# Attention in a one-core decoder kernel: turning the scaled numerators alone, and adding the turned queries behind the turn

## The chip, the cores and the metric

The kernel runs on one core of one Trainium2 chip. A core has five engines with queues of their own: TensorE (PE, with its weight loads shown as PEld), VectorE (DVE), ScalarE (ACT), GpSimd (POOL) and SyncE (SP, which here issues DMAs). They meet through semaphores. The metric is the time on the device in microseconds, as the median of several runs; lower is better.

## What is computed

A decoder block over x of shape (16, 112, 256) and a context of shape (16, 375, 256): four RWKV layers, a cross attention with softmaxed queries and keys, and eight gated experts. The change lies in the cross attention:

```
q = softmax(heads(x @ Wq.T + bq), axis=-1)
k = softmax(heads(y @ Wk.T + bk), axis=-1)
v = heads(y @ Wv.T + bv)
k_cumsum = sum(k, axis=-2, keepdims=True)
D_inv = 1.0 / sum(q * k_cumsum, axis=-1, keepdims=True)
kv = einsum("bhnd,bhne->bhde", k, v)
out = q + einsum("bhnd,bhde->bhne", q, kv) * D_inv
return out @ Wp.T + bp
```

There are 16 batches of 112 queries, 16 heads of 16 columns, 256 channels.

## The kernel before

Every engine has one program, written out by hand in a fixed order, and a semaphore wait stands wherever one engine needs another. An instruction that waits holds back all that is behind it in its engine's queue.

The attention part (attention_phase) runs a loop over the 16 batches n. In each round the context of a batch is projected to keys and values, the keys are softmaxed (VectorE: maxima L1178, arguments L1182; ScalarE: exponential L1410; VectorE: sum, reciprocal and product, L1187 to L1189), and TensorE forms the product of keys and values (keys_values, L1575) in the bank kvp, which VectorE copies into block diagonal matrices (L1156, L1158). The queries go in groups c of four batches (G = 4). stage(n) gives the place i = n % 4, the group c1 whose queries are being made and the group c2 = c1 - 1 whose attention is being made. For a group c2 the steps are:

- round i = 3 of the queries' own group: TensorE turns the queries q into the bank qbanks (q_turned), and ScalarE copies them to qt (L1399). They are turned so that they can be the stationary side of the next products.
- round i = 0: TensorE forms denominators (L1530) and numerators (L1535, into abanks); VectorE takes the reciprocal of the denominators (L1232).
- round i = 1: VectorE scales the numerators to num (L1239) and adds them to the queries, q (L1241). Then it makes the arguments of the next group's queries (L1216, L1220). TensorE, at the end of its round, turns the sum into abanks (turn_out, L1512), and ScalarE copies it to ot (L1403).
- round i = 2: TensorE projects ot with wp into abanks (project_out, L1519 and the bias L1474).
- round i = 3: VectorE adds the result to x (L1245), and the statistics of a layer norm follow.

ot is the same memory as xt, which holds the turned x for the query projection, so its rows in a profile bear the name xt. Behind round 15 a tail finishes the last group beside the first products of the experts (times_up: hf, L1820; low_h: hl, L1827; silu, L1925). From about 896 us TensorE works through the experts.

Of the kernel before, what the change touches and what calls it, by code (L numbers as in the profile page):

```python
# [8 lines left out]
ACT = mybir.ActivationFunctionType  # L9
# [3 lines left out]
B, T, C = 16, 112, 256  # L13
L, F = 4, 1024
CB = C // P
G = 4
# [948 lines left out]
def attention_phase(nc, g, io, ctx):  # L965
# [6 lines left out]
    with tiles:  # L972
# [133 lines left out]
        def vector(dve):  # L1106
            steps = [0]

            def did(ins):
                ins.then_inc(dve_step, 1)  # L1110
                steps[0] += 1
                return steps[0]

            def after(n):
                dve.wait_ge(dve_step, n)
# [7 lines left out]
            def heads(t):  # L1123
                return t.rearrange("p t (h d) -> p (t h) d", d=D)

            def head_banks(banks):
                return banks[0:T].rearrange("p i (h d) -> p (i h) d", d=D)

            def spread(t):
                return t[:].unsqueeze(2).broadcast_to([t.shape[0], t.shape[1], D])  # L1130
# [82 lines left out]
            def q_arguments(c):  # L1213
                qc = q[c % 2][:]
                dve.wait_ge(q_done, c + 1)
                after(did(dve.tensor_reduce(qtop[:], head_banks(qbanks), AX.X, ALU.max)))  # L1216
                if c >= 2:

                    dve.wait_ge(o_turned, CB * (c - 1))
                dve.tensor_tensor(heads(qc), head_banks(qbanks), spread(qtop), ALU.subtract).then_inc(qarg_ready, 1)  # L1220

            def q_normalise(c):
# [10 lines left out]

            def attend(c):

                qc = q[c % 2][:]
                dve.wait_ge(den_read, c + 1)
                dve.wait_ge(num_done, c + 1)
                after(did(dve.tensor_tensor(heads(num[:]), head_banks(abanks), spread(drec), ALU.mult)))  # L1239
                dve.wait_ge(q_turned, CB * (c + 1))  # L1240
                dve.tensor_tensor(qc, qc, num[:], ALU.add).then_inc(o_ready, 1)  # L1241

            def add_attention(c):
                dve.wait_ge(pj_done, c + 1)
# [27 lines left out]
            def groups():  # L1272

                times_up, low_h, combine_arguments, combine_weights, experts = g["expert"]["vector"](dve)
                dve.wait_ge(mask_set, 3)
                for n in range(B):
                    i, c1, c2 = stage(n)
                    k_arguments(n)
                    if n == 0:
                        output_bias()  # L1280
                    if n:
                        block_diagonals(n - 1)
                    if i == 0 and c1 is not None:
                        add_input(c1)
                    if i == 2 and c1 is not None:
                        q_normalise(c1)
                    if i == 3 and c2 is not None:
                        add_attention(c2)
                    k_normalise(n)
                    if n + 2 < B:  # L1290
                        low_context(n + 2)
                    if i == 0 and c1 is not None:
                        rsqrt(1, c1)
                    if i == 0 and c2 is not None:
                        denominators(c2)
                    if i == 1 and c2 is not None:
                        attend(c2)
                    if i == 1 and c1 is not None:
                        q_arguments(c1)
                    if i == 3 and c2 is not None:  # L1300
                        rsqrt(2, c2)
                    if n in SPLITS:
                        low_weights(SPLITS.index(n))
                    if i == 2 and n in TURNS:
                        low_x2(TURNS.index(n))
                last = GROUPS - 1
                times_up(0, 0, 0)
                times_up(0, 0, 1)
                block_diagonals(B - 1)
                low_h(0, 0)  # L1310
                low_x2(last - 1)
                denominators(last)
                attend(last)
                for n in (2, 3):
                    times_up(0, 0, n)
                    low_h(0, n - 1)
                add_attention(last)
                times_up(0, 1, 0)
                low_h(0, 3)
                rsqrt(2, last)  # L1320
                times_up(0, 1, 1)
                low_h(0, 4)
                low_x2(last)
                times_up(0, 1, 2)
                low_h(0, 5)
                times_up(0, 1, 3)
                combine_arguments()
                low_h(0, 6)
                combine_weights()
                experts()  # L1330
# [3 lines left out]
        def scalar(act):  # L1334
# [57 lines left out]
            def groups():  # L1392

                silu, high_h, combine_exp, experts = g["expert"]["scalar"](act)
                last = GROUPS - 1

                def q_turned_out(c):
                    act.wait_ge(q_turned, CB * (c + 1))
                    act.activation(qt[c % 2][:], qbanks[:, :, 0:G * T], ACT.Copy).then_inc(qt_ready, 1)  # L1399

                def o_turned_out(c):
                    act.wait_ge(o_turned, CB * (c + 1))
                    act.activation(ot[:], abanks[:, :, 0:G * T], ACT.Copy).then_inc(ot_ready, 1)  # L1403

                act.wait_ge(const_set, 4)
                v_out(0)
                for n in range(B - 1):
                    i, c1, c2 = stage(n)
                    act.wait_ge(arg_ready, n + 1)
                    act.activation(k[n % 2][:], k[n % 2][:], ACT.Exp).then_inc(exp_ready, 1)  # L1410
                    if n in TURNS:
                        x2_out(TURNS.index(n))
                        high_x2(TURNS.index(n))
                    if n + 2 < B:
                        high_context(n + 2)
                    if i == 0 and c1 is not None:
                        rsqrt0(1, c1)
                    if i == 3 and c2 is not None:
                        rsqrt0(2, c2)
                    if i == 3 and c1 is not None:  # L1420
                        q_turned_out(c1)
                    v_out(n + 1)
                    if i == 1 and c1 is not None:
                        act.wait_ge(qarg_ready, c1 + 1)
                        act.activation(q[c1 % 2][:], q[c1 % 2][:], ACT.Exp).then_inc(qexp_ready, 1)
                    if i == 1 and c2 is not None:
                        o_turned_out(c2)
                    if i == 0 and c1 is not None:
                        normalise(1, c1, x1_ready)
                        act.wait_ge(x1_turned, CB * (c1 + 1))  # L1430
                        act.activation(xt[:], qbanks[:, :, 0:G * T], ACT.Copy).then_inc(xt_ready, 1)
                    if i == 3 and c2 is not None:
                        normalise(2, c2, x2_ready)
                    if n + 1 in SPLITS:
                        high_weights(SPLITS.index(n + 1))
                act.wait_ge(arg_ready, B)
                act.activation(k[(B - 1) % 2][:], k[(B - 1) % 2][:], ACT.Exp).then_inc(exp_ready, 1)
                q_turned_out(last)
                rsqrt0(2, last - 1)
                silu(0, 0, 0)  # L1440
                normalise(2, last - 1, x2_ready)
                silu(0, 0, 1)
                high_h(0, 0)
                x2_out(last - 1)
                high_x2(last - 1)
                silu(0, 0, 2)
                high_h(0, 1)
                o_turned_out(last)
                silu(0, 0, 3)
                high_h(0, 2)  # L1450
                silu(0, 1, 0)
                high_h(0, 3)
                rsqrt0(2, last)
                normalise(2, last, x2_ready)
                silu(0, 1, 1)
                high_h(0, 4)
                act.wait_ge(g["r_done"], 1)
                logits_out(act, kvp, g, EARLY)
                x2_out(last)
                high_x2(last)  # L1460
                silu(0, 1, 2)
                high_h(0, 5)
                silu(0, 1, 3)
                act.wait_ge(g["r_done"], 2)
                logits_out(act, kvp, g, LATE)
                high_h(0, 6)
                combine_exp()
                experts()
# [3 lines left out]
        def tensor(pe):  # L1472
# [83 lines left out]

            def turn_out(c):
                pe.wait_ge(o_ready, c + 1)
                turn(abanks, q[c % 2], o_turned)

            def project_out(c):
                pe.wait_ge(ot_ready, c + 1)
# [587 lines left out]
```

## Time and profile before

| | us |
|---|---|
| runs | 1817.99, 1819.19, 1819.70 |
| median | 1819.19 |
| the profiled execution | 1819.54 |
| its span | 1817.5 |
| TensorE busy | 1730.9 (95%) |
| VectorE busy | 1222.5 (67%) |
| ScalarE busy | 986.7 (54%) |

The times of a profile are counted from the start of its span; the 2 us beside it lie around the program. A timeline row says when an instruction, or a row of like ones, started, how long it took, on which engine and line of the kernel, and what it wrote from what. In square brackets is the time that the engine had been idle before it, with the instruction that released it. The ends of matmuls are modelled. VectorE and ScalarE start an instruction that doesn't depend on the one before shortly before that one's end.

### The profile page before, as it was taken

To read this page: it belongs to the slowest core of one execution; us is meant where nothing else is said; L and a number is where in the kernel's file an instruction comes from. 1 tells how busy PE (TensorE), PEld (TensorE's weight loads), DVE (VectorE), ACT (ScalarE), POOL (GpSimd) and SP (SyncE) were. 2 spreads that over 40 slices of the span, in tenths; PEclk is the share of its full clock that TensorE was granted. 3 is DMA by queue.
4 is the path that set the end of the run, shared out by engine and by line. 5 is a ranking of instruction groups with operands and counts; after the bars stand their busy time and mean duration, and the time that the engine had idled before them with its cause. 6 is when DMAs were issued, how large, how long until landed. Compare 5 with 4: busy or idle time off the path is not lost.

```text
span 1817.5 us, 27302 instructions
## 1 busy us (share of the span) xinstructions
PE 1730.9 (95%) x10508; PEld 1514.4 (83%) x10508; DVE 1222.5 (67%) x1897; ACT 986.7 (54%) x1516; POOL 18.6 (1%) x42
## 2 busy tenths in 40 slices
PE   3599999999999898989999999999999999999997
PEld 1388888878888788988899989998899989999896
DVE  6989999999999856998454544444454444545446
ACT  4789998998999773455533332333332333333324
POOL 1000000000000000000000000000000000000000
PEclk9699999999999999999999999999999999999999
DMA  7301110011011002111111001110111101020001
GB/s 187 58 1 30 24 59 18 18 29 65 12 24 41 1 29 90 45 55 50 52 36 36 27 9 35 35 35 0 35 35 35 35 0 35 35 75 0 1 1 41
DMA packets 37966, 64.79 MB, mean 36 GB/s; under 512 B 3286, under 2 KB 22012, under 8 KB 36860
## 3 DMA queue, kind: packets, MB, share of 16 engines
q1 hardware_dynamic: 34620, 55.47, 9.4%
q0 software_dynamic: 3264, 8.19, 3.0%
q8 instruction: 55, 0.90, 0.2%
q14 instruction: 27, 0.22, 0.0%
HBM read 59.99 MB, written 3.67 MB: 35 GB/s over the span
## 4 chain that ended last, share of the span: by engine, by line
PE 82%; DVE 8%; ACT 6%; issue 2%; DMA 2%; SPq 0%; ACTq 0%; POOL 0%; DVEq 0%; POOLq 0%
PE fbank L1998 34%; PE fbank L2020 17%; PE pair L882 8%; PE pair L867 7%; PE pair L842 7%; PE pair L852 5%; PE proj L1480 2%; PE pair L832 1%; ACT kf L659 1%; ACT kfh L661 1%; DMA wckl<-in_w_ck 1%; PE qbanks L1519 1%; PE abanks L1519 1%; DMA x<-in_ln_b 1%; ACT kf L657 1%
## 5 line engine op out<-in xcount | busy, mean ns | idle before, releaser
L1820 DVE TENSOR_TENSOR hf<-sil,fbank 128x512 f32<-128x512 f32 (+1 forms) x256 | 158.9, 621 | 478.9 <-PE fbank L1998 407.3
L1925 ACT ACTIVATE sil<-fbank 128x512 f32<-128x512 f32 (+1 forms) x256 | 139.3, 544 | 614.6 <-PE fbank L1998 614.6
L1998 PE MATMUL fbank<-xh,wh 128*128 128x512 f32 (+1 forms) x1024 | 290.0, 365 | 1.2 <-ACT sil L1925 1.2
L1998 PE MATMUL fbank<-xh,wl 128*128 128x512 f32 (+1 forms) x1024 | 288.9, 363 | 0.0
L1998 PE MATMUL fbank<-xl,wh 128*128 128x512 f32 (+1 forms) x1024 | 288.8, 363 | 0.0
L2020 PE MATMUL fbank<-wl,hh 128*128 128x256 f32 x896 | 250.3, 279 | 0.0
L2020 PE MATMUL fbank<-wh,hh 128*128 128x256 f32 x896 | 250.2, 279 | 0.0
L2020 PE MATMUL fbank<-wh,hl 128*128 128x256 f32 x896 | 250.1, 279 | 0.0
L1998 PEld LDWEIGHTS fbank<-xl,wh 128*128 128x128 f32 x1024 | 184.6, 189 | 30.9
L1998 PEld LDWEIGHTS fbank<-xh,wl 128*128 128x128 f32 x1024 | 184.4, 189 | 30.3
L1998 PEld LDWEIGHTS fbank<-xh,wh 128*128 128x128 f32 x1024 | 180.6, 189 | 27.8 <-ACT sil L1925 1.6
L2020 PEld LDWEIGHTS fbank<-wl,hh 128*128 128x128 f32 x896 | 168.3, 188 | 2.1
L2020 PEld LDWEIGHTS fbank<-wh,hh 128*128 128x128 f32 x896 | 168.4, 188 | 1.8
L2020 PEld LDWEIGHTS fbank<-wh,hl 128*128 128x128 f32 x896 | 168.4, 188 | 0.0
L1827 DVE TENSOR_TENSOR hl<-hf,hh 128x512 fp32r<-128x512 f32 (+1 forms) x256 | 158.3, 618 | 0.0
L882 PE MATMUL pair<-wcvh,kfh 128*112 128x256 f32 x512 | 147.2, 287 | 0.0
L1918 ACT ACTIVATE hh<-hf 128x512 fp32r<-128x512 f32 (+1 forms) x256 | 146.3, 571 | 0.5 <-DVE hf L1820 0.5
L882 PE MATMUL pair<-wcvh,kfl 128*112 128x256 f32 x512 | 143.3, 280 | 0.0
L882 PE MATMUL pair<-wcvl,kfh 128*112 128x256 f32 x384 | 107.6, 280 | 0.0
L882 PEld LDWEIGHTS pair<-wcvh,kfh 128*112 128x112 f32 x512 | 89.8, 175 | 0.7
L882 PEld LDWEIGHTS pair<-wcvh,kfl 128*112 128x112 f32 x512 | 89.8, 175 | 0.0
L1844 DVE SCALAR_TENSOR_TENSOR acc<-fbank,cw,acc 128x256 f32<-128x256 f32 x210 | 87.5, 477 | 0.0
(240 smaller groups left out, 3096.8 us busy)
## 6 DMA issues: line engine op xcount, KB each, us to landing
raw<-in_w_gate SPq DMA_DIRECT2D x16, 512.0 KB, 3.8
raw<-in_w_up SPq DMA_DIRECT2D x16, 512.0 KB, 4.7
raw<-in_w_down SPq DMA_DIRECT2D x16, 512.0 KB, 5.8
raw<-in_w_ck SPq DMA_DIRECT2D x4, 1024.0 KB, 6.6
raw<-in_w_cv SPq DMA_DIRECT2D x4, 1024.0 KB, 6.9
wcvl<-in_w_cv POOLq DMA_DIRECT2D x6, 512.0 KB, 5.4
raw<-in_ctx_t SPq DMA_DIRECT2D x4, 750.0 KB, 5.9
ct<-in_ctx_t SPq DMA_DIRECT2D x4, 750.0 KB, 4.9
```

Source lines behind the costliest of these rows:

```text
L842: ins = pe.matmul(pair[BANKS[name]][:, o, 0:G * T], w[:, b, o * P:(o + 1) * P], mixed[name][:, b].rearrange("p g t -> p (g t)"), start=b = ...
L852: ins = pe.matmul(banks[0:T, i // 2, (i % 2) * C:(i % 2 + 1) * C], src[:, b, i, :], w[:, b, :], start=b == 0, stop=b == CB - 1)
L867: ins = pe.matmul(banks[:, i, 0:G * T], w[b], a[:, b, :], start=n == 0, stop=n == 3 * CB - 1)
L882: ins = pe.matmul(pair[3][0:T, i // 2, (i % 2) * C:(i % 2 + 1) * C], a[:, i * T:(i + 1) * T], w, start=j == n == i % 2 == 0, stop=j == FT ...
L1480: ins = pe.matmul(proj[0:ST, out, :], a[s % 2][:, b, t * ST:(t + 1) * ST], w[:, b, cols], start=n == 0, stop=n == 3 * CB - 1 and cols.star ...
L1820: dve.tensor_tensor(hf[i][:, 0:w], sil[i][:, 0:w], banks(e, t, f)[1][:, 0:w], ALU.mult).then_inc(hf_ready, 1)
L1827: dve.tensor_tensor(hl[t % 2][:, f, 0:w], hf[f % 2][:, 0:w], hh[t % 2][:, f, 0:w], ALU.subtract)\
L1844: ins = dve.scalar_tensor_tensor(a, ps, w, a, ALU.mult, ALU.add)
L1918: act.activation(hh[t % 2][:, f, 0:w], hf[f % 2][:, 0:w], ACT.Copy).then_inc(hh_ready, 1)
L1925: act.activation(sil[f % 2][:, 0:w], banks(e, t, f)[0][:, 0:w], ACT.Silu).then_inc(sil_ready, 1)
L1998: ins = pe.matmul(banks(e, t, f)[k][:, 0:w], m[h][:, o:o + P], a[:, b, columns(c)], start=i == 0, stop=i == 3 * CB - 1)
L2020: ins = pe.matmul(bank[4 + 2 * (t % 2) + i // 2][:, (i % 2) * C:(i % 2 + 1) * C], a[t % 2][:, f, i * P:(i + 1) * P], m[h][:, DOWN + f * C: ...
```

## The change

The queries are no longer added before the turn. VectorE scales the numerators to num, and TensorE turns num alone. Since the queries lie turned in qt already, VectorE then adds qt to the turned numerators out of abanks and writes ot itself (add_query, with 128 x 896 elements). ScalarE's copy o_turned_out is gone. Four waits follow from that:

- the scaling of a group waits until num has been turned for the group before (o_turned);
- the new addition waits for the turn (o_turned) and for the copy of the queries (qt_ready);
- the arguments of a later group's queries wait for q_turned where they waited for o_turned;
- ScalarE's copy of the turned queries waits for the addition that read that buffer last (ot_ready).

```
@@ vector: q_arguments
-                    dve.wait_ge(o_turned, CB * (c - 1))
+                    dve.wait_ge(q_turned, CB * (c - 1))
@@ vector: attend
-                qc = q[c % 2][:]
                 dve.wait_ge(den_read, c + 1)
                 dve.wait_ge(num_done, c + 1)
-                after(did(dve.tensor_tensor(heads(num[:]), head_banks(abanks), spread(drec), ALU.mult)))
-                dve.wait_ge(q_turned, CB * (c + 1))
-                dve.tensor_tensor(qc, qc, num[:], ALU.add).then_inc(o_ready, 1)
+                if c:
+                    dve.wait_ge(o_turned, CB * c)
+                dve.tensor_tensor(heads(num[:]), head_banks(abanks), spread(drec), ALU.mult).then_inc(o_ready, 1)
+            def add_query(c):
+                dve.wait_ge(o_turned, CB * (c + 1))
+                dve.wait_ge(qt_ready, c + 1)
+                dve.tensor_tensor(ot[:], abanks[:, :, 0:G * T], qt[c % 2][:], ALU.add).then_inc(ot_ready, 1)
@@ vector: groups
                     if i == 1 and c1 is not None:
                         q_arguments(c1)
+                    if i == 1 and c2 is not None:
+                        add_query(c2)
...
                 attend(last)
-                for n in (2, 3):
-                    times_up(0, 0, n)
-                    low_h(0, n - 1)
+                times_up(0, 0, 2)
+                add_query(last)
+                low_h(0, 1)
+                times_up(0, 0, 3)
+                low_h(0, 2)
@@ scalar
                     act.wait_ge(q_turned, CB * (c + 1))
+                    if c >= 2:
+                        act.wait_ge(ot_ready, c - 1)
                     act.activation(qt[c % 2][:], qbanks[:, :, 0:G * T], ACT.Copy).then_inc(qt_ready, 1)
-                def o_turned_out(c):
-                    act.wait_ge(o_turned, CB * (c + 1))
-                    act.activation(ot[:], abanks[:, :, 0:G * T], ACT.Copy).then_inc(ot_ready, 1)
...
-                    if i == 1 and c2 is not None:
-                        o_turned_out(c2)
...
-                o_turned_out(last)
@@ tensor: turn_out
-                turn(abanks, q[c % 2], o_turned)
+                turn(abanks, num, o_turned)
```

VectorE's queue in round 5, where group 0 has its place i = 1; acl is the low half of a context, the k and top rows belong to the keys of the next batch. Before:

```order
L1169 TENSOR_TENSOR acl<-ct,ach 128x2x375 [waits proj_done,acth_ready]
L1239 TENSOR_TENSOR num<-abanks,drec 112x1024 [waits num_done,den_read]
L1241 TENSOR_TENSOR q<-q,num 112x1024 [waits q_turned,adve_step]
L1216 TENSOR_REDUCE qtop<-qbanks 112x64 [waits q_done]
L1220 TENSOR_TENSOR q<-qbanks,qtop 112x1024 [waits adve_step]
L1178 TENSOR_REDUCE top<-proj 125x48 [waits v2_ready,proj_done]
L1182 TENSOR_TENSOR k<-proj,top 125x768 [waits kv_done,adve_step]
```

and now:

```order
L1169 TENSOR_TENSOR acl<-ct,ach 128x2x375 [waits proj_done,acth_ready]
L1241 TENSOR_TENSOR num<-abanks,drec 112x1024 [waits num_done,den_read]
L1216 TENSOR_REDUCE qtop<-qbanks 112x64 [waits q_done]
L1220 TENSOR_TENSOR q<-qbanks,qtop 112x1024 [waits adve_step]
L1247 TENSOR_TENSOR xt<-abanks,qt 128x896 [waits qt_ready,o_turned]
L1178 TENSOR_REDUCE top<-proj 125x48 [waits v2_ready,proj_done]
L1182 TENSOR_TENSOR k<-proj,top 125x768 [waits kv_done,adve_step]
```

The addition has moved from ahead of the query arguments to behind them, right ahead of the next batch's maxima, and waits there for TensorE's turn.

VectorE's queue in the tail, group 3; hf and hl are the experts' hidden values and their low half. Before:

```order
L1232 RECIPROCAL drec<-kvp 112x64 [waits den_done]
L1239 TENSOR_TENSOR num<-abanks,drec 112x1024 [waits num_done,den_read]
L1241 TENSOR_TENSOR q<-q,num 112x1024 [waits q_turned,adve_step]
L1820 TENSOR_TENSOR hf<-sil,fbank 128x512 [waits hh_ready,hl_ready,gu_done,sil_ready]
L1827 TENSOR_TENSOR hl<-hf,hh 128x512 [waits hh_ready]
```

and now:

```order
L1232 RECIPROCAL drec<-kvp 112x64 [waits den_done]
L1241 TENSOR_TENSOR num<-abanks,drec 112x1024 [waits o_turned,num_done,den_read]
L1826 TENSOR_TENSOR hf<-sil,fbank 128x512 [waits hh_ready,hl_ready,gu_done,sil_ready]
L1247 TENSOR_TENSOR xt<-abanks,qt 128x896 [waits qt_ready,o_turned]
L1833 TENSOR_TENSOR hl<-hf,hh 128x512 [waits hh_ready]
```

Here the addition stands behind the first of the two products. TensorE's queue keeps its order; its turns read num where they read q.

## Rows read from the trace of the kernel before

**Rows 1.** The page's busy times, and busy times of 760 to 780 us
```profile
PE 1730.9 (95%) x10508; PEld 1514.4 (83%) x10508; DVE 1222.5 (67%) x1897; ACT 986.7 (54%) x1516; POOL 18.6 (1%) x42
...
core 0: us, PE busy (x) PEld busy (x) DVE busy (x) ACT busy (x) POOL busy (x), PEclk, DMA share, GB/s
...
760.00:780.00 20.00, 18.80 (x147) 17.78 (x146) 19.52 (x31) 10.39 (x19) 0.00 (x0) 1.00 0.17 52
```

**Rows 2.** Timeline of VectorE, group 0: start, duration, line, out<-in
```profile
752.87 1.22 DVE L1239 TENSOR_TENSOR num<-abanks,drec 112x1024 f32<-112x1024 f32 x1
754.12 1.23 DVE L1241 TENSOR_TENSOR q<-q,num 112x1024 f32<-112x1024 f32 x1
755.26 1.22 DVE L1216 TENSOR_REDUCE qtop<-qbanks 112x64 f32<-112x1024 f32 x1
756.51 1.23 DVE L1220 TENSOR_TENSOR q<-qbanks,qtop 112x1024 f32<-112x1024 f32 x1
757.65 0.95 DVE L1178 TENSOR_REDUCE top<-proj 125x48 f32<-125x768 f32 x1
```

**Rows 3.** Timeline of TensorE, group 0: the turn, and the projection's first products
```profile
757.68 0.93 PE L1512 MATMUL abanks<-ident,q 112*128 112x112 f32 x8
...
759.89 1.02 PE L1519 MATMUL abanks<-wp,xt 128*112 128x256 f32 x4
```

**Rows 4.** Timeline of TensorE, behind group 0: two waits for VectorE
```profile
774.47 1.61 PE L1575 MATMUL kvp<-v,k 125*128 125x129 f32 x12 [0.55 <-DVE k L1189]
...
785.49 1.60 PE L1575 MATMUL kvp<-v,k 125*128 125x129 f32 x12 [0.59 <-DVE drec L1232]
```

**Rows 5.** Timelines of VectorE and TensorE, group 1
```profile
797.82 0.95 DVE L1178 TENSOR_REDUCE top<-proj 125x48 f32<-125x768 f32 x1
...
807.60 0.94 DVE L1169 TENSOR_TENSOR acl<-raw,ach 128x750 fp32r<-128x750 f32 x1 [2.10 <-ACT ach L1382]
...
797.84 0.93 PE L1512 MATMUL abanks<-ident,q 112*128 112x112 f32 x8
```

**Rows 6.** Timelines of VectorE and TensorE, group 2
```profile
841.17 0.95 DVE L1178 TENSOR_REDUCE top<-proj 125x48 f32<-125x768 f32 x1
...
847.89 0.96 DVE L1189 TENSOR_TENSOR k<-k,rec 125x768 f32<-125x768 f32 x1
850.24 1.09 DVE L1253 TENSOR_TENSOR xl<-acc,xh 128x896 fp32r<-128x896 f32 x1 [1.40 <-ACT xh L1367]
851.52 0.96 DVE L1178 TENSOR_REDUCE top<-proj 125x48 f32<-125x768 f32 x1 [0.19 <-PE proj L1474]
...
841.20 0.93 PE L1512 MATMUL abanks<-ident,q 112*128 112x112 f32 x8
...
858.92 0.73 PE L1998 MATMUL fbank<-xh,wh 128*128 128x512 f32 x2 [1.19 <-ACT sil L1925]
```

**Rows 7.** Timelines of VectorE and TensorE, the tail with group 3
```profile
869.82 0.69 DVE L1820 TENSOR_TENSOR hf<-sil,fbank 128x512 f32<-128x512 f32 x1 [0.27 <-PE fbank L1998]
...
869.60 0.99 PE L1512 MATMUL abanks<-ident,q 112*128 112x112 f32 x8
...
873.18 1.02 PE L1519 MATMUL abanks<-wp,xt 128*112 128x256 f32 x4
```

**Rows 8.** By tile: durations in ns (min/median/max), first and last start, forms
```profile
L1239 DVE TENSOR_TENSOR num<-abanks,drec x4: 1217/1218/1225, 752.9 to 867.1; 112x1024 f32<-112x1024 f32 x4
L1403 ACT ACTIVATE xt<-abanks x4: 902/902/920, 758.7 to 870.6; 128x896 f32<-128x896 f32 x4
...
L1253 DVE TENSOR_TENSOR xl<-acc,xh x4: 1085/1093/1093, 809.6 to 890.5; 128x896 fp32r<-128x896 f32 x4
```

**Rows 9.** TensorE's granted clock (PEclk) in stretches, and rows before and in one
```profile
705.79 1.90 PE L1575 MATMUL kvp<-v,k 125*128 125x129 f32 x12 [3.02 <-DVE k L1189]
709.62 1.75 PE L1512 MATMUL qbanks<-ident,x 112*128 112x112 f32 x8 [1.93 <-ACT x L1354]
...
708.00:712.00 4.00, 2.38 (x12) 2.39 (x13) 1.70 (x4) 2.16 (x5) 0.00 (x0) 0.50 0.00 0
...
814.00:818.00 4.00, 2.29 (x19) 2.08 (x19) 3.90 (x7) 2.22 (x6) 0.00 (x0) 1.00 0.02 4
```

## The prediction

> **What bounds the kernel now.** I read the page first, then the busy time by stretches, then the timelines of VectorE and TensorE. TensorE is busy for 95% of the span, and in most of the kernel an operation of another engine costs nothing. The attention part (roughly 700 to 880 us) is different: between 760 and 780 us VectorE is busy for 19.52 of 20 us and TensorE for 18.80 [rows 1]. There VectorE is the queue that is never empty, and TensorE waits for it: 0.55 us ahead of the key-value products of one batch, 0.59 us ahead of those two batches on [rows 4]. So the changed operations are to be judged by one question: does VectorE stand still where nothing else is late?
>
> The part works on batches n = 0 to 15, and every fourth batch carries the attention of one group of four (c2). I call the places n = 5, 9, 13 and the tail after batch 15 groups 0 to 3. All four numbers follow from them.
>
> **What goes away.** VectorE's sum q + num, 1.23 us at group 0, four times in all [rows 2], and ScalarE's copy of the turned sum, 0.90 us, four times [rows 8]. ScalarE is busy only half of 760 to 780 us (10.39 of 20) [rows 1]; it may start the next exponential 0.9 us earlier, but VectorE would have to hand it the arguments first, so I cost this relief at nothing. The sum also made TensorE's turn wait, but the turn starts at 757.68, over 2 us after the sum's end at 755.35 [rows 2, 3]: TensorE comes to it in its own order, behind a solid row of products, and an earlier num does not move it. So neither removal reaches TensorE.
>
> **What comes instead.** An addition on VectorE of 128 x 896 elements, from PSUM (the turned numerators) and SBUF (the turned queries). The nearest row is the subtraction of the same 896 columns, 1.09 us [rows 8]; I take it. A floor is ScalarE's copy of the same tile, 0.90, a ceiling the product num with 1024 columns out of PSUM, 1.22 [rows 8]. VectorE's work alone thus falls by 0.14 us a group, a gain far below what matters.
>
> The Trainium skill ("VectorE: DVE Perf Modes", section on the TRN2 errata) gives VectorE 62 cycles more for a PSUM source than for an SBUF source, about 0.065 us at its 0.96 GHz. The trace doesn't agree: num, read out of PSUM, takes 1.22 us and the sum of the same size out of SBUF 1.23 [rows 2, 8]. By the page's rule the addition would take 1.16 and the total below would be 2.5 instead of 2.3 us.
>
> **The new wait, group 0.** The addition needs TensorE's turn, and it stands in VectorE's queue ahead of the maxima and arguments of the next batch (L1178, L1182), on which ScalarE's exponential, then everything of that batch, hangs.
> 1. num starts at 752.87 as before. The two query operations follow it directly: an operation without a wait starts 1.14 us after one of this size (754.12 to 755.26) [rows 2]. So they start at 754.01 and 755.15, and the second is over by 756.4. Even with 0.1 us of doubt VectorE is out of work by 756.5.
> 2. The turn ends at 757.68 + 0.93 = 758.61 [rows 3]. The addition starts at about 758.64. VectorE has stood still for 2.2 us.
> 3. It ends at 759.73. The next operation may start 0.09 us before that (as L1178 at 757.65 before the end of L1220 at 757.74 [rows 2]), so at 759.64. In the kernel before it started at 757.65. **VectorE is 2.0 us later.**
> 4. The projection that reads the result has its first product at 759.89, weights a little before [rows 3]. The result is there at 759.73; the margin is 0.1 us. I count 0.05 us for this, 0 to 0.1.
>
> Is anything slack enough to absorb 2.0 us? VectorE has no idle time in its timeline from 752.87 until after 785.5: the rows that follow carry no wait. TensorE starts with slack, but it is used up at 774.47, where it already waited for VectorE, and it waits again at 785.49 [rows 4]. From there on TensorE, and with it ScalarE and the next x turn, are 2.0 us late as a whole. Term: **+2.0**.
>
> **Group 1.** The same shape, everything shifted. In the old clock the next L1178 started at 797.82 and the turn ended at 797.84 + 0.93 = 798.77, so the addition starts at 798.80 and L1178 at 799.80: 1.98 us late [rows 5]. But here VectorE later waits 2.10 us for ScalarE's copy of the context (L1169 at 807.60) [rows 5]. That copy follows TensorE's turn of x2, which is in TensorE's own order. 1.98 fits into 2.10, with 0.12 to spare. What passes is the 0.05 by which the projection may start late. Term: **+0.05**.
>
> **Group 2.** L1178 was at 841.17 and the turn ends at 841.20 + 0.93 = 842.13; the addition starts at 842.16, L1178 at 843.16: 1.99 us late [rows 6]. The row of VectorE operations up to the normalised keys moves from 847.89 to 849.88 and gives way at 850.75 (0.96 less 0.09 later). Then came a wait of 1.40 us for ScalarE, until 850.24, of which 0.51 us of lateness is left. Behind the 1.09 us subtraction L1178 starts at 851.75 instead of 851.52, since a further wait of 0.19 is used up [rows 6]. The remainder reaches the SiLU through the statistics and ScalarE, for which TensorE waited 1.19 us at 858.92 [rows 6]. Term: **+0.25**.
>
> **Group 3, the tail.** Now VectorE has room. The turn ends at 869.60 + 0.99 = 870.59; the product hf at 869.82 stands ahead of the addition and is over by 870.51; the addition runs 870.62 to 871.71, and the projection needs it at 873.18 [rows 7]. Behind it the low half waits 1.2 us, for sums that are far off. The expert part then is TensorE's own row. Term: **0**.
>
> **Sum.** 2.0 + 0.05 + 0.25 = **+2.3 us**. The profiled execution took 1819.54 us (its span is 1817.5), so a profile of the changed kernel should take 1821.8. It stood 0.35 above the median of 1819.19; on the median I forecast **1821.5**, which is +0.13%. A measurement of this kernel can tell about 0.2%, 3.6 us, from no change, so this counts as the same. With the addition at 0.90 us the first and third group give 0.2 less each (+1.9), with 1.22 each of three groups gives 0.13 more (+2.7).
>
> **Rivals.**
> - *A: the stall leaks in all three groups (slower).* In group 1 only 0.12 us separates 1.98 from 2.10, and in group 2 the slack is 1.59. If what VectorE waits for there (ScalarE's copies) were itself moved by the late operations, each group would cost its 2.0. 3 x 2.0 = +6.0, 1825.2. It decides when the context copy of batch 12 waits for something of VectorE's; against it, the copy follows TensorE's turn, which needs only x2 and a bank. 12%.
> - *B: TensorE's clock falls in the new gaps (slower).* In this trace TensorE idled for 3.02 us, worked, idled again for 1.93, and the granted clock was 0.50 from 708 to 712 us, half of 2.4 GHz. Eight transposes took 1.75 us there [rows 9], against 0.93 [rows 3]; 4 us at half the clock leave 2.0 us of work undone. In the changed kernel the 0.55 before 774.47 grows to at most 2.55. Against it: the clock stayed 1.00 from 814 to 818 us with TensorE busy for only 2.29 of 4 us [rows 9]. Price 2.0, giving +4.3, 1823.5; it decides at a granted clock below 1 between 774 and 790 us. 12%. The Trainium skill ("TensorE: Matmul & The Clock Gate", Part 1) says that the throttled state is the default and activity releases it. By that rule a longer idle piece is the danger here, and the rows at 708 us agree.
> - *C: the stall is covered.* If VectorE's lateness at 774.47 were made good, by waits that I take for its own but are another's, only the 0.3 of groups 1 and 2 would be left: 1819.5. Against it stand two waits of TensorE for VectorE. 11%.
> - *D: faster.* The turn comes forward by the whole 1.23 us of the sum in each of three groups, because TensorE's order is looser than it looks, and VectorE follows: 3 x 1.23 = 3.7, 1815.5. The turn stood behind TensorE's solid row [rows 3], so 3%.
>
> **How the numbers follow.** The forecast has 62%. Its own range is 1820.3 to 1822.8, with the duration of the addition (1.9 to 2.7) and half a microsecond of scatter of the medians (three runs lay between 1818.0 and 1819.7). Of the 62 I give 6 to a result just over +0.2%. Slower: 6 + 12 + 10 (most of B) = 28%. Faster: 3%. The same: 56 + 2 + 11 = 69%. For 8 in 10 the range takes in C and B: 1819.0 to 1824.0.
>
> **What would show it.** In the profile of the changed kernel: the addition, 1.09 us each, with an idle time of about 2.2 us before it, released by the turn, in group 0; about the same in groups 1 and 2, and ScalarE's copy gone. VectorE's L1169 behind group 1 without its wait of 2.10. TensorE's waits at 774.47 grown to between 1 and 2.5 us. The start of the expert part 2.3 us later, and from there no difference. I am wrong if VectorE doesn't wait before the addition, if the start of group 1's batch is not 2 us late, or if the lateness grows past 830 us.

## The result, and the profile after

The changed kernel takes 1824.14 us, the median of 12 runs, against 1820.04 us for the kernel before in 12 runs. The ratio is 1.0019 with a 95% interval of 1.0011 to 1.0027, that is +3.5 us (2.0 to 4.9); the two medians themselves lie 4.1 us apart. The loss is small but clear of noise. The forecast was +2.3 us on a median of 1819.19; by the ratio alone that median would have become 1822.7. The kernel before was itself 0.85 us slower in these 12 runs than in the three behind the forecast.

The page of the changed kernel hardly differs from [rows 1]:

```profile
span 1820.1 us, 27300 instructions
PE 1731.7 (95%) x10508; PEld 1517.0 (83%) x10508; DVE 1221.5 (67%) x1897; ACT 983.2 (54%) x1512; POOL 18.6 (1%) x42
```

VectorE has 1.0 us less to do, ScalarE 3.5 us less with its four copies gone, and the span is 2.6 us longer. Both engines have less work and the kernel is slower, so the loss is waiting, or work that runs at a lower clock.

Next, the timelines of the places in [rows 2 to 6], as the changed kernel has them. Columns are start, duration, line, what is written from what, and the idle time ahead with its releaser. VectorE at group 0:

```profile
751.66 1.22 DVE L1241 TENSOR_TENSOR num<-abanks,drec 112x1024 f32<-112x1024 f32 x1
752.79 1.21 DVE L1216 TENSOR_REDUCE qtop<-qbanks 112x64 f32<-112x1024 f32 x1
754.04 1.22 DVE L1220 TENSOR_TENSOR q<-qbanks,qtop 112x1024 f32<-112x1024 f32 x1
757.44 1.09 DVE L1247 TENSOR_TENSOR xt<-abanks,qt 128x896 f32<-128x896 f32 x1 [2.18 <-PE abanks L1518]
758.45 0.95 DVE L1178 TENSOR_REDUCE top<-proj 125x48 f32<-125x768 f32 x1
```

TensorE at group 0, its turn and the projection behind it, and then the wait that grew:

```profile
756.47 0.93 PE L1518 MATMUL abanks<-ident,num 112*128 112x112 f32 x8
...
758.68 1.03 PE L1525 MATMUL abanks<-wp,xt 128*112 128x256 f32 x4
...
775.26 1.61 PE L1581 MATMUL kvp<-v,k 125*128 125x129 f32 x12 [1.71 <-DVE k L1189]
```

From num to the next L1178 VectorE takes 758.45 - 751.66 = 6.79 us, where it took 757.65 - 752.87 = 4.78 in [rows 2]: 2.01 us more, all of it the idle time of 2.18 ahead of the addition. TensorE keeps its distance of 2.21 us from the turn to the projection, as in [rows 3], so the projection doesn't wait. Its wait for VectorE's keys has grown from 0.55 [rows 4] to 1.71.

VectorE at groups 1 and 2:

```profile
799.60 1.09 DVE L1247 TENSOR_TENSOR xt<-abanks,qt 128x896 f32<-128x896 f32 x1 [2.17 <-PE abanks L1518]
...
808.40 0.94 DVE L1169 TENSOR_TENSOR acl<-raw,ach 128x750 fp32r<-128x750 f32 x1
...
842.96 1.09 DVE L1247 TENSOR_TENSOR xt<-abanks,qt 128x896 f32<-128x896 f32 x1 [2.17 <-PE abanks L1518]
...
851.55 1.08 DVE L1259 TENSOR_TENSOR xl<-acc,xh 128x896 fp32r<-128x896 f32 x1
```

The same stall stands in both groups, and the waits that stood later in [rows 5] (2.10) and [rows 6] (1.40) are gone: one wait has been exchanged for the other.

One thing that no changed operation explains stands in the tail. Here are, for the changed kernel, TensorE's denominators and numerators of group 3, and the granted clock of 5 us around them (PEclk, the number ahead of the last two columns; 1.00 is 2.4 GHz and 0.50 is 1.2 GHz):

```profile
864.39 1.74 PE L1536 MATMUL kvp<-kcm,qt 128*112 128x8 f32 x16 [0.57 <-DVE kcm L1158]
865.98 3.59 PE L1541 MATMUL abanks<-kvbd,qt 128*112 128x128 f32 x16
...
865.00:870.00 5.00, 5.00 (x31) 4.92 (x31) 1.89 (x3) 0.75 (x1) 0.00 (x0) 0.66 0.05 16
```

and both in the kernel before:

```profile
864.97 1.98 PE L1535 MATMUL abanks<-kvbd,qt 128*112 128x128 f32 x16
...
865.00:870.00 5.00, 5.00 (x34) 4.26 (x34) 3.97 (x5) 1.12 (x2) 0.00 (x0) 1.00 0.00 2
```

The sixteen products take 3.59 us instead of 1.98. The clock went from 2.4 to 1.2 GHz in the middle of a row of work.

This is the account for the two profiles, each stretch taken from one num to the next and from the last num to the first product of the experts' down projection (896.52 us before, 899.11 after; both rows stand behind this table):

| stretch | before | after | difference | forecast |
|---|---|---|---|---|
| start to num of group 0 | 752.87 | 751.66 | -1.21 | 0 |
| to num of group 1 | 40.16 | 42.16 | +2.00 | +2.0 |
| to num of group 2 | 43.35 | 43.36 | +0.01 | +0.05 |
| to num of group 3 | 30.68 | 32.49 | +1.81 | +0.25 |
| to the experts' first sum | 29.46 | 29.44 | -0.02 | 0 |
| from there to the end of the span | 920.98 | 920.99 | +0.01 | 0 |

The first product of that sum, in the kernel before and then in the changed one:

```profile
896.52 0.37 PE L2020 MATMUL fbank<-wh,hh 128*128 128x256 f32 x1
```

```profile
899.11 0.37 PE L2026 MATMUL fbank<-wh,hh 128*128 128x256 f32 x1
```

The first line of the table is no effect of the change, which touches nothing there. Executions of one kernel reach this point at different times: the kernel before at 752.87 and, in a second profile further down, at 755.14. From group 0 on it is 143.65 us before and 147.45 after, +3.80. I use this length, "num to experts", for every profile below, since it leaves that scatter out.

### The profile page after: what moved, and what is told of

Its sections match the earlier page's. It is cut to its first block, busy times and chain, and to the rows that moved or that the text cites. A ratio compares the mean times of both kernels' runs of the same rounds, so it can differ in the third digit from the quotient of the medians.

```text
span 1820.1 us, 27300 instructions
## 1 busy us (share of the span) xinstructions
PE 1731.7 (95%) x10508; PEld 1517.0 (83%) x10508; DVE 1221.5 (67%) x1897; ACT 983.2 (54%) x1512; POOL 18.6 (1%) x42
## 4 chain that ended last, share of the span: by engine, by line
PE 82%; DVE 8%; ACT 6%; issue 2%; DMA 1%; SPq 0%; ACTq 0%; POOL 0%; DVEq 0%; POOLq 0%
PE fbank L2004 34%; PE fbank L2026 17%; PE pair L882 8%; PE pair L867 7%; PE pair L842 7%; PE pair L852 5%; PE proj L1486 2%; PE pair L832 1%; PE qbanks L1525 1%; ACT kf L659 1%; ACT kfh L661 1%; PE kvp L1581 1%; DMA wckl<-in_w_ck 1%; ACT kf L657 1%; DMA x<-in_ln_b 1%
```

## The experiments

Two questions were open. Is VectorE's standing still the cost, and only where it has no slack? And what is the 1.6 us in the tail? In what follows "the fall" is the clock's fall at group 3's numerators. The theories are S (the stall, priced as forecast), L (the stall leaks in every group), W (the work moved to VectorE or a late projection is the cost), and C (the clock).

**Moving the addition.** In e1_add_later the addition of groups 0 to 2 stands behind the next batch's maxima and arguments:

```
@@ vector: groups
                     k_arguments(n)
+                    if i == 2 and c2 in (0, 1, 2):
+                        add_query(c2)
...
-                    if i == 1 and c2 is not None:
-                        add_query(c2)
```

> The changed kernel, but in rounds 5 to 13 VectorE's addition of the turned queries stands behind the next batch's maxima and arguments (L1178, L1182) instead of ahead of them; nothing is left out. Theory S (VectorE's standing still ahead of the addition is the cost): VectorE no longer idles, the addition starts when the turn ends, and the time is that of the kernel before or 0.1 to 0.3 us less (ratio to before 0.9995 to 1.0003). Rival W (the work moved from ScalarE to VectorE, or the late projection, is the cost): the time stays 2 to 4 us above before. Rival C (part of the cost is a fall of TensorE's clock in the tail around 866 us, not tied to the stall): some 1.5 us above before remain, ratio 1.0008.

Measured: 1.0001 (0.9992 to 1.0010), and 143.72 us from num to experts. The addition's idle time fell from 2.18 to 0.16:

```profile
760.58 0.96 DVE L1182 TENSOR_TENSOR k<-proj,top 125x768 f32<-125x768 f32 x1
761.70 1.09 DVE L1247 TENSOR_TENSOR xt<-abanks,qt 128x896 f32<-128x896 f32 x1 [0.16 <-PE abanks L1518]
762.70 0.41 DVE L1156 TENSOR_TENSOR kvbd<-kvp,mask 128x256 f32<-128x256 f32 x1
```

The idle time is 0.16 us in groups 1 and 2 as well. The whole loss is gone, with the same work on the same engines. W is refuted, and the loss hangs on the place of one instruction in VectorE's queue. The tail's fall of the clock was gone too, which I had not expected.

**One group at a time.** e2_group0_only keeps the addition of group 0 where the change has it and moves those of groups 1 and 2 as above; e8_groups12_only does the opposite.

```
@@ e2: vector, groups (e8: the two sets exchanged)
+                    if i == 2 and c2 in (1, 2):
+                        add_query(c2)
...
-                    if i == 1 and c2 is not None:
+                    if i == 1 and c2 in (0,):
                         add_query(c2)
```

> The changed kernel, with the addition of groups 1 and 2 moved behind the next batch's maxima and arguments; in group 0 it stays ahead of them; nothing is left out. Theory S: +2.0 us over before (VectorE idle 2.2 us ahead of the addition in group 0 alone), and 0.25 us less than the changed kernel. Rival L (each group's stall leaks): only a third of the changed kernel's loss, 1.1 to 1.4 us over before. Rival C: as S, and 1.6 us more where the profile has TensorE's clock at half around 866 us.

> The changed kernel, with the addition of group 0 moved behind the next batch's maxima and arguments; in groups 1 and 2 it stays ahead of them; nothing is left out. Theory S: VectorE idles 2.2 us ahead of the addition in groups 1 and 2, but only 0.25 us of it reach the end, and with the 0.15 us that e1_add_later had in group 0 that makes +0.4 us. No fall of the clock in the tail. Rival L (leak): +4 us.

Measured: e2 1.0020 (1.0011 to 1.0029) and 147.20 us, +3.55. e8 1.0002 (0.9993 to 1.0011) and 143.89 us, +0.24. So two stalls of 2.17 us cost a quarter of a microsecond. The one stall of 2.18 us comes with the rest, which holds the 1.6 us of the fall. L is refuted. e2 carries the fall of the clock in its tail, e8 doesn't. L1543 is the numerators' line in both, e2 first:

```profile
868.66 3.28 PE L1543 MATMUL abanks<-kvbd,qt 128*112 128x128 f32 x16
```

```profile
864.75 1.98 PE L1543 MATMUL abanks<-kvbd,qt 128*112 128x128 f32 x16
```

**The wait without the change.** e3_wait_only is the kernel before with one wait more.

```
@@ vector: groups
                     if i == 1 and c1 is not None:
                         q_arguments(c1)
+                    if i == 1 and c2 is not None:
+                        dve.wait_ge(o_turned, CB * (c2 + 1))
```

> The kernel before, with one wait more: in rounds 5, 9 and 13 VectorE waits for TensorE's turn (o_turned) ahead of the next batch's maxima, where the changed kernel has its addition; nothing is left out. Theory S: VectorE is late by the idle time alone. The turn ended at 758.61 where L1178 started at 757.65, so +1.0 us in group 0; in groups 1 and 2 the same 1.0 us fits into waits of 2.10 and 1.40 us, so +1.0 us in all. Rival L: 3 x 1.0 = +3.0 us. Rival C: +1.0, and 1.6 more where the clock falls around 866 us.

Measured: 1.0007 (0.9998 to 1.0016), and 144.68 us, +1.03. The timed runs alone can't tell this from no change; the profile can. It is S to 0.03 us, with the old arithmetic: the wait alone costs, in group 0 alone. L would have been +3. No fall in the tail.

**Filling TensorE's wait in the tail.** The fall at 866 us came after a wait of 1.42 us at 859.94 (1.19 in [rows 6]). e4_fill_after puts nine matmuls into it (in the kernel they stand in a helper of their own; here they are written out in place).

```
@@ tensor: gate_up, ahead of the second group of products, once
+                pe.wait_ge(bd_ready, 2 * (B - 1))
+                for b in range(3):
+                    for t in range(STILES):
+                        pe.matmul(kvp[:, 0:P + 1], k[0][:, t, 0:P], v[0][:, t, 0, :], start=t == 0, stop=t == STILES - 1)
                 pe.wait_ge(sil_ready, n)
```

> The changed kernel, and nine matmuls more on TensorE in its wait for the SiLU at 858 to 860 us (they write again into the bank of the key-value products, which is overwritten afterwards); nothing is left out. Rival C (the profile of the changed kernel had TensorE's clock at half from 866 to 869 us, after a wait of 1.42 us, and the numerators took 3.45 instead of 1.83 us): with that wait filled the clock stays whole there and the time is 1.0 to 1.6 us less than that of the changed kernel, about 2.3 us above before. Theory S alone (the clock's fall there was an accident of one profile): no gain, 0 to 0.2 us more than the changed kernel.

Measured: 1.0019 (1.0010 to 1.0028), and 147.50 us. (The 3.45 and 1.83 us of the expectation are the same two rows of numerators in another view, which starts counting 0.15 us later.) The filling ran in the wait, and the fall came all the same; the first row is the nine added matmuls, which the profile counts as 18:

```profile
858.03 2.17 PE L1593 MATMUL kvp<-v,k 125*128 125x129 f32 x18
...
865.65 3.65 PE L1541 MATMUL abanks<-kvbd,qt 128*112 128x128 f32 x16
```

So this gap is not what brings the fall. It was there in every profile with the full stall in group 0 so far, and in none without. Two readings were left: a long wait of TensorE behind group 0 brings it, or the tail's place in time does.

**A pure delay, short and long.** e6_delay2_before and e7_delay3_before are the kernel before with 2.5 and 3.75 us of repeated VectorE work beside group 0; e9_delay3_after is the changed kernel with the latter.

```
@@ vector: q_arguments (2 in e6, 3 in e7 and e9)
+                for _ in range(2 if c == 1 else 0):
+                    after(did(dve.tensor_reduce(qtop[:], head_banks(qbanks), AX.X, ALU.max)))
                 after(did(dve.tensor_reduce(qtop[:], head_banks(qbanks), AX.X, ALU.max)))
```

> The kernel before, with VectorE's maxima of the queries (L1216) taken twice more ahead of group 1's query arguments, 2 x 1.25 = 2.5 us of VectorE beside group 0 and nowhere else; nothing is left out, and the changed kernel's addition is not in it. Theory P (a pure delay of 2.0 to 2.5 us in front of the tail makes TensorE's clock fall to half around the numerators of group 3, for 1.6 us more): the profile has a granted clock of 0.50 there, the numerators of group 3 take over 3 us instead of 1.83, and the time is 2.5 + 1.6 = 4.1 us over before. Rival A (the fall belongs to the changed kernel's own operations or waits): +2.5 us, clock 1.00 from 865 to 885 us.

> As e6_delay2_before, but three more maxima, 3 x 1.25 = 3.75 us of VectorE beside group 0. Theory P with the place of the tail in time as the cause (it falls where it meets a moment at which the chip lowers the clock, and a later tail misses that moment): no fall around group 3, +3.75 us, no more than e6_delay2_before. Theory P with the length of TensorE's waits as the cause (a longer delay, a lower clock): the fall is there too, and the time is 3.75 + 1.6 = 5.4 us over before.

> The changed kernel, with the maxima L1216 taken three times more ahead of group 1's query arguments: 3.75 us of VectorE work beside group 0, of which 2.2 fit into its idle time ahead of the addition, so 1.6 us of new delay; nothing is left out. Place in time as the cause: the tail is 3.8 us later than in the kernel before, misses the fall, and the time is 3.8 us over before, the same as the changed kernel without the extra work. Length of the waits, or the changed kernel's own operations, as the cause: the fall stays, 5.4 us over before.

Measured: e6 1.0031 (1.0019 to 1.0043) and 149.83 us, +6.18. Here 2.5 are the delay, about 1.6 the row at half clock, and the rest is a second fall near 892 us that lasted 6.8 us instead of 3.4. (Every profile of this case, that of the kernel before included, has a fall between 887 and 899 us; outside e6 it lasts 3.4 or 3.5 us and so cancels in the comparisons.) e7 in its profile has 147.46 us, +3.81, with 1.25 us more of delay and 2.4 us less of time. e9 has 1.0022 (1.0013 to 1.0031) and 147.33 us, +3.68: 1.6 us of delay more than the changed kernel, and not longer. The numerators of e6, then of e7, then of e9:

```profile
868.32 3.40 PE L1537 MATMUL abanks<-kvbd,qt 128*112 128x128 f32 x16
```

```profile
870.12 1.98 PE L1537 MATMUL abanks<-kvbd,qt 128*112 128x128 f32 x16
```

```profile
868.56 1.98 PE L1543 MATMUL abanks<-kvbd,qt 128*112 128x128 f32 x16
```

e9's TensorE waits at least as long as the changed kernel's behind group 0 (1.25 us ahead of the projection, then 1.72 ahead of the keys' products), and has no fall. The length of the waits is out; in the profiles so far, delays of 2.0 to 2.5 us in front of the tail have the fall, and 0 to 1.0 and 3.7 don't. The timed runs of e7 don't fit its profile: 1.0034 (1.0022 to 1.0045), some 2 us above it, and so no faster than e6 with the shorter delay.

**The same kernels again.** Three kernels were profiled once or twice more, without an edit.

> The kernel before, unchanged, for a second profile. Place in time as the cause: no fall of TensorE's clock between 860 and 885 us, num of group 0 to the first expert sum 143.6 us as in the first profile. If the fall came by chance: it may be there.

> The changed kernel, unchanged, for a second profile. Place in time as the cause: the fall around group 3's numerators is there again and num of group 0 to the first expert sum takes 147.4 us. If it came by chance: it may be missing, with 145.9 us.

> The changed kernel, unchanged, for a third profile. The kernel before showed two kinds of execution: from group 0's num to the first expert sum 143.65 us with the clock whole in the tail, and 145.31 us with a fall there, the latter with a longer fall at 706 to 716 us. If the changed kernel has both kinds too, a profile with the long fall at 706 us may show another length than 147.4 us: 145.9 us if the tail then misses the fall, 147.5 if not. If this execution has the short fall at 706 us, it repeats 147.4 us.

> The kernel of e7_delay3_before, unchanged, for a second profile, because its timed runs lay 5.6 to 6.2 us over before where its profile had 3.8 us more from group 0 on. If another execution of it has a second fall of the clock (TensorE waited 3.42 us ahead of the projection of group 0), it shows as 0.50 beside 765 to 780 us; if not, the part from group 0 on is 3.8 us longer again and the rest comes from ahead of it.

Measured: the changed kernel has 147.47 and 147.43 us, with the fall both times, so three times of three. The kernel before has 145.31 us this time, with the fall:

```profile
865.64 1.97 PE L1530 MATMUL kvp<-kcm,qt 128*112 128x8 f32 x16 [0.57 <-DVE kcm L1158]
867.46 3.42 PE L1535 MATMUL abanks<-kvbd,qt 128*112 128x128 f32 x16
```

That is 1.66 us more than in its first profile, and the expectation for it was wrong: the kernel before can have the fall with no delay at all. There is an earlier difference between the two executions. Near 706 us (705.3 to 710.4) the clock falls in every profile, and here it stayed low for 10.2 us instead of 6.8, which makes the work behind it later. The first row is that execution, the second the first profile:

```profile
712.00:716.00 4.00, 4.00 (x19) 3.88 (x19) 1.32 (x2) 2.76 (x4) 0.00 (x0) 0.50 0.00 0
```

```profile
712.00:716.00 4.00, 4.00 (x22) 3.65 (x21) 2.85 (x4) 2.37 (x4) 0.00 (x0) 0.78 0.02 4
```

e12_delay3_again has 150.57 us, 3.1 us more than the first profile of the same kernel, with two falls that e7 didn't have, at 764 to 768 and at 870 to 874 us. The first came 1.4 us behind a wait of TensorE of 3.41 us, ahead of the projection of group 0; e7 had the same wait, 3.42 us, and no fall there.

```profile
764.00:768.00 4.00, 4.00 (x14) 3.11 (x13) 3.86 (x6) 1.95 (x4) 0.00 (x0) 0.57 0.00 0
...
870.00:874.00 4.00, 4.00 (x20) 3.86 (x21) 1.90 (x3) 0.00 (x0) 0.00 (x0) 0.57 0.00 0
```

Together the lengths from num to experts. The last column is the time from the moment at which the clock fell near 706 us (read in stretches of 0.1 us) to the first product of group 3's numerators:

| kernel | us | over 143.65 | fall | numerators behind the fall near 706 |
|---|---|---|---|---|
| before, first profile | 143.65 | 0 | no | 158.0 |
| before, second | 145.31 | +1.66 | yes | 160.9 |
| e1, addition later everywhere | 143.72 | +0.07 | no | 158.3 |
| e8, groups 1 and 2 stalled | 143.89 | +0.24 | no | 158.5 |
| e3, wait alone | 144.68 | +1.03 | no | 158.9 |
| e2, group 0 stalled | 147.20 | +3.55 | yes | 160.0 |
| changed kernel, three profiles | 147.45, 147.47, 147.43 | +3.8 | yes, each | 160.3, each |
| e4, wait in the tail filled | 147.50 | +3.85 | yes | 160.4 |
| e9, changed and delayed | 147.33 | +3.68 | no | 161.9 |
| e7, before and delayed, first | 147.46 | +3.81 | no | 161.7 |
| e12, the same again | 150.57 | +6.92 | yes, and one more | 163.5 |
| e6, before and less delayed | 149.83 | +6.18 | yes, and a longer one at 892 | 160.9 |

This column sorts the profiles where the delay doesn't. Numerators that start 158.0 to 158.9 us behind the earlier fall run at full clock, those at 160.0 to 160.9 us meet the fall, the second profile of the kernel before among them, and those at 161.7 and 161.9 us miss it. Only e12 has another fall in between. In the seven profiles at 160.0 to 160.9 us the fall itself starts 160.4 or 160.5 us behind the earlier one, whichever kernel it is. So the place in time that goes with the fall is the one against the clock's earlier fall; against the start of the span the numerators don't sort (868.16 and 868.56 us without the fall, 868.32 and 868.66 with it). The sorting was found in these profiles, and no further run was made to test it. Nor do the batches of runs exclude the chip as a part of the cause: e1 to e4 ran on one, e6 to e9 on another, e10 to e12 on a third, and all three profiles of the third have the fall; on each of the first two some have it and some don't.

## Why the prediction was right, and where it was not

It forecast a small loss inside what counts as the same, and the size of the stall and its path were right; one term of its sum was not. One of its own signs of being wrong came true: the lateness grew past 830 us, from 2.01 us at group 2's num to 3.82 at group 3's, and most of that growth is the fall. That the spans of the first two profiles lie 2.6 us apart, close to the forecast 2.3, is luck: 1.21 us of scatter ahead of group 0 hid most of the 1.6 us of the fall.

- **What goes away is worth nothing.** Right. The turn's place in TensorE's row didn't move, ScalarE's relief didn't show, and e1 with the same removals stands at the time of before.
- **The addition, 1.09 us.** Right, 1.09 four times. Out of PSUM it takes what the subtraction out of SBUF takes, 1.09 [rows 8]. The Trainium skill ("VectorE: DVE Perf Modes", section on the TRN2 errata) adds 62 cycles for a PSUM source; the trace doesn't agree here either.
- **Group 0, +2.0.** Right: +2.00 between two nums, VectorE idle for 2.18 us where 2.2 was said. The 0.05 for a late projection wasn't needed; it started without a wait.
- **Group 1, +0.05.** Right: +0.01. The 2.10 of slack took the lateness of 2.00 (800.61 - 793.82 = 6.79 from num to the next L1178, before 4.79) with little left, as the vanished wait at L1169 shows.
- **Group 2, +0.25.** Right. L1259 came 0.51 us late against num (851.55 - 837.18 = 14.37, before 13.86), and what reached the TensorE row that waits for the SiLU (859.94 us, behind a wait of 1.42) was 859.94 - 837.18 - (858.92 - 836.38) = 0.22.
- **Group 3, 0.** Right for VectorE: the addition at 873.17 stands behind hf, and the projection isn't late. But this is the term that failed as a sum for the stretch. It took for granted that TensorE's row runs at full clock there, and the sixteen numerators took 3.59 us instead of 1.98. That is the 1.6 us between the 2.25 us that the stalls explain and the 3.80 in the profile.
- **Rival B** had the mechanism (TensorE's clock falls, for some 2 us) with the wrong place and the wrong trigger. It looked at 774 to 790 us, behind the wait that grew; there the clock stayed at 1.00, and e4 and e9 show that longer or shorter waits don't decide it.
- **Rival A** is refuted by e8 and e3, **C** by e2 and by group 0's +2.00, **D** by the turn's unmoved place (4.81 us behind num in both kernels).
- **The forecast's own range**, 1820.3 to 1822.8, is 0.3 and 0.4 us wider than the two parts it names: they give 1819.19 + 1.9 - 0.5 = 1820.6 and 1819.19 + 2.7 + 0.5 = 1822.4.

The measured +3.5 us lies near 2.25 + 1.6 = 3.85. It may well be less than that since the kernel before has the fall too in some executions (one profile of two), while the changed kernel had it in three of three; how often each has it in the timed runs isn't known, so the split of the 3.5 us is shown for profiles and only argued for the median. The profiles order the fall by the tail's place behind the earlier fall, but don't tell why that place decides. What TensorE did just before this fall, the sixteen denominators of 8 columns each, it did in the profiles without the fall too; whether they have a part in it no run here tested. The Trainium skill ("TensorE: Matmul & The Clock Gate", Part 1) says that the clock is given by the recent activity of the array; the rows agree in that waits stand ahead of the fall, but TensorE counts as busy at 865 us in the rows with the fall and in those without.

## What to carry to other kernels

When work moves to another engine, its place in that engine's queue counts for more than its length: the addition costs nothing behind the next batch's arguments and 2.0 us ahead of them, because there it waits for another engine at the head of the queue that bounds the stage, and with that the tail moved to where TensorE's clock was low, for 1.6 us more. Price a new wait by following its lateness to the next wait of the same engine that another releases: of three equal stalls of 2.2 us here, two were swallowed by slack of 2.10 and 1.59 us. And for effects of 0.1 to 0.2%, compare stretches between two marks in the traces, over more than one profile, before a microsecond is given to a cause.

## What the hardware showed that I had not expected

- A delay can cost more than itself, and a longer one less. 2.5 us of VectorE work in group 0 lengthened the kernel before by 6.2 us in its profile, 3.75 us of it by 3.8, since TensorE's clock at half meets the tail in the one and not in the other. Repeated, the latter gave 6.9, and in the timed runs the two kernels are equal within noise (1.0031 and 1.0034). Nor do e9's timed runs settle it: 1.0022 (1.0013 to 1.0031) beside the changed kernel's 1.0019 agrees with its profile, but doesn't exclude the 1.6 us of added delay.
- The granted clock fell to half in an unbroken row of products (0.66 over 865 to 870 us, TensorE busy for 5.00 of 5), with the last wait ahead of it (0.57 us) the same in the kernel without the fall. The kernel before has such a place too, behind forty products of 16 columns and eight transposes (clock 0.50, TensorE busy for 3.00 of 3 us):

```profile
882.57 4.53 PE L52 MATMUL kvp<-wrt,acc 128*128 128x16 f32 x40
...
888.00:891.00 3.00, 3.00 (x8) 2.32 (x8) 1.79 (x3) 2.94 (x6) 0.00 (x0) 0.50 1.03 259
```

- Executions of one and the same kernel differ by it: 143.65 and 145.31 us from num to experts for the kernel before, 147.46 and 150.57 for e7 and e12. The expert part of the first two profiles shows no such difference: 920.98 and 920.99 us.
